# Two convolution layers with group norm: channels on partitions, 32x32 TensorE tiles over pixel pairs

## The chip, the cores and the metric

The kernel runs on one core of one Trainium2 chip. The metric is the device time of one launch in microseconds (us), lower is better. TensorE (PE) multiplies, VectorE (DVE), ScalarE (ACT) and GpSimd (POOL) work beside it, and SyncE (SP) issues transfers. Everything is fp32.

## What is computed

The input is 64 images of 256 x 256 pixels with 16 channels (268 MB). Two layers follow each other; each is a group norm over 8 groups of two channels (statistics over the whole image), a 3x3 convolution whose kernel is a product of small factors, a bias, a relu and a residual sum:

```python
def _L0_conv_ref(inputs, u, v, w, b):
    kern = jnp.einsum('lj,lk,li->ijkl', u, w, v)
    out = lax.conv_general_dilated(inputs, kern, window_strides=(1, 1), padding='SAME', ...)
    return jax.nn.relu(out + b)
...
x = x + _L0_conv_ref(_gn(x), L0_conv_u, L0_conv_v, L0_conv_w, L0_conv_b)
x = x + _L1_conv_ref(_gn(x), L1_conv_u, L1_conv_v, L1_conv_w, L1_conv_b)
```

## The kernel before

The partition is an image row; an image is two halves of 128 rows, and a row holds 256 pixels of 16 channels. Four images lie in SBUF (`image`, 4 MB each). A job is one layer of one image, 128 jobs in all, two images taken in turn, so that the norm of one job is worked out during another. The jobs of a group of four images are written out, and the group is looped over 16 times.

A job has a row stage and a band stage. The row stage has 18 tiles (NT), nine for each half. For a tile, TensorE transposes four windows of eight pixels (L271), so that pixel and channel come onto the partitions; ScalarE applies the norm's scale and bias on the way out of PSUM (L355); TensorE multiplies by `mix`, the horizontal taps and the channel mix (L285); DVE (two tiles of three, L423) or ScalarE (L370) copies the result to `z`. The band stage has 16 products with a 128x128 band matrix over rows, one for each channel, of 512 columns each (L320), whose PSUM ScalarE takes out with relu and bias (L398), and one step of four small rows at the seam between the halves (L314, two products with 64 rows and 32 columns of the array, into neighbouring column groups). Between jobs DVE adds the relu to the image (L434, 16 adds) and takes statistics for the next norm (L445, 16); these fill DVE's queue between the copies of the row stage. A norm ends in a product with ones (L329) and some ten small DVE steps (L459 to L484) with one root on ScalarE (L345).

TensorE's queue is in program order: two tiles' transposes run ahead, then the row step of a tile, then the bands. The PSUM buffers are two for transposes, two for row products and three for bands. At L281 and L269 TensorE's sequencer waits for a buffer by an instruction of its own. An image is loaded in one transfer of 4 MB (L230, L365) and stored in one (L360). An fp32 product or row of the profile is two pairs of weight load and matmul records, a transpose one pair.

Of the kernel before, what the change touches and what calls it, by code (L numbers as in the profile page):

```python
# [8 lines left out]
P = 128  # L29
HALVES = H // P  # L30
GN_GROUPS = 8
EPS = 1e-5
TAPS = 3
LAYERS = 2
PX = P // C
SPAN = PX + 2
BANK = 512
BUFS = 4
JOBS = BUFS * LAYERS
GROUPS = IMAGES // BUFS  # L40

TILES_W = []
_start = 0
while _start < W:
    _windows = [s for s in range(_start, _start + 4 * PX, PX) if s < W]
    _end = _windows[-1] + PX
    TILES_W.append((_start + (_start > 0), W - 1 if _end == W else _end - 2, _windows))
    _start = W if _end == W else _end - 2  # L50
TILES = [(half, *t) for half in range(HALVES) for t in TILES_W]
NT = len(TILES)

T_SLOTS = 3
PS_T, PS_Z, PS_B = 2, 2, 3
LOAD_AT = 6
STORE_AT = 3
EARLY = 2
SEAM_AT = 9
STAT_AT, ROOT_AT = 10, 12  # L60
BANDS = list(range(C))
BANDS.insert(SEAM_AT, "seam")
NB = len(BANDS)
ADD_PX = 32
ADDS = HALVES * W // ADD_PX
STATS = HALVES * GN_GROUPS
FILL_FROM = 3
FILL_A = 24
PARAMS = C + 2 * TAPS * C + C + TAPS + 1
SEAM_PARTS = 2  # L70
SEAM_W = W // SEAM_PARTS


def on_scalar(i):

    return i % 3 == 2


ZA = sum(on_scalar(i) for i in range(NT))
ZV = NT - ZA  # L80


def z_before(i, scalar):

    return sum(on_scalar(n) == scalar for n in range(i + 1))


def layer_of(k):
    return k % 4 // 2


def buf_of(k):
    return 2 * (k // 4) + k % 2


def build(nc, x, params, shifts, spans, seams, pick, out):
# [5 lines left out]
    x_rows = x.rearrange("n (s p) w c -> n p s (w c)", p=P)  # L102
    out_rows = out.rearrange("n (s p) w c -> n p s (w c)", p=P)

    with ExitStack() as ctx:
# [8 lines left out]
        R = sb("relu", [P, C, HALVES, W])  # L114
        T = sb("transposed", [P, T_SLOTS, BANK])
        band = [sb(f"band{y}", [P, C, P]) for y in range(LAYERS)]
        mix = [sb(f"mix{y}", [P, SPAN, C]) for y in range(LAYERS)]
        seam_w = [sb(f"seam_w{y}", [P, P]) for y in range(LAYERS)]
        par = [sb(f"parameters{y}", [P, PARAMS]) for y in range(LAYERS)]
        shift = sb("shift", [P, TAPS, P])  # L120
        span = sb("span", [P, TAPS, SPAN])
        pick_s = sb("pick", [P, 2, GN_GROUPS])
        ones = sb("ones", [P, P])
        seam_z = sb("seam_z", [P, W])
        seam_r = sb("seam_r", [SEAM_PARTS * 2 * C, SEAM_W])
        bn = sb("bn", [P, STATS, 2, 3])
        squares = sb("squares", [P, STATS, 2])
        sums = sb("sums", [P, 2, GN_GROUPS])
        picked = sb("picked", [P, 2, GN_GROUPS])
        moments = sb("moments", [P, 2])  # L130
        small = sb("small", [P, 6])
        norm = sb("norm", [P, 2, 2])

        seam_mask = Z[:, 0:1, :, :].rearrange("p l s w -> p (l s w)")[:, 0:TAPS * P].rearrange(
            "p (i m) -> p i m", i=TAPS)
        z_flat = Z[:, 1:1 + LAYERS, :, :].rearrange("p l s w -> p l (s w)")
        mixed = [z_flat[:, y, 0:TAPS * C].rearrange("p (j l) -> p j l", j=TAPS) for y in range(LAYERS)]
        part = [z_flat[:, y, TAPS * C:(TAPS + SPAN) * C].rearrange("p (q l) -> p q l", q=SPAN)
                for y in range(LAYERS)]
        scratch = [R[:, 4 * y:4 * y + 4, :, :].rearrange("p l s w -> p (l s w)").rearrange(  # L140
            "p (l m) -> p l m", l=C) for y in range(LAYERS)]

        ps_t = [ctx.enter_context(nc.psum_tensor(f"ps_t{i}", [P, BANK], fp32)) for i in range(PS_T)]
        ps_z = [ctx.enter_context(nc.psum_tensor(f"ps_z{i}", [P, BANK], fp32)) for i in range(PS_Z)]
        ps_b = [ctx.enter_context(nc.psum_tensor(f"ps_b{i}", [P, BANK], fp32)) for i in range(PS_B)]
        ps_s = ctx.enter_context(nc.psum_tensor("ps_s", [P, BANK], fp32))

        const_in = sem("const_in")
        image_in = [sem(f"image_in{b}") for b in range(BUFS)]
        image_out = [sem(f"image_out{b}") for b in range(BUFS)]  # L150
        ones_set = sem("ones_set")
        built = sem("built")
        set_step = sem("set_step")
        set_step_pool = sem("set_step_pool")
        turned = sem("turned")
        normed = sem("normed")
        z_made = sem("z_made")
        z_vector = sem("z_vector")
        z_scalar = sem("z_scalar")
        seam_in = sem("seam_in")  # L160
        banded = sem("banded")
        relued = sem("relued")
        seam_out = sem("seam_out")
        added = sem("added")
        stat_step = sem("stat_step")
        stat_sums = sem("stat_sums")
# [400 lines left out]
```

## Time and profile before

| | us |
|---|---|
| median of 3 runs | 5744.07 (5743.53 to 5744.48) |
| the profiled execution | 5745.21 |
| its span, first to last instruction | 5743.4 |
| TensorE busy | 5165.1 (90%) |
| DVE busy | 4424.2 (77%) |
| ScalarE busy | 3427.1 (60%) |

The page gives busy time by engine, the chain of work that ended last, and groups of instructions by line. In a row, x is a count, "mean ns" the recorded length of one (for TensorE with the time until its result has landed, so records overlap), and the idle time is that of the engine just ahead of such instructions, with what ended it. PE is TensorE's matmul, PEld its weight load and PEldq its sequencer.

### The profile page before, as it was taken

The numbers are of one execution on the slowest core, as the hardware profiler recorded it, in microseconds if no ns is written. First come the engines' busy times: TensorE is split into PE (matmuls) and PEld (weight loads), VectorE is DVE, ScalarE is ACT, GpSimd is POOL, SyncE is SP. The second block draws the span as 40 slices with busy tenths as digits, with TensorE's granted clock in tenths as the row PEclk, the third lists the DMA queues.
The fourth block names the chain that finished last, engine by engine and source line by source line (L and its number), as shares of the span: only waits on it lengthen the run. The fifth ranks groups of instructions, "written<-read, shape, count | busy, mean of one in ns | idle before, by whom it ended". The sixth has DMA issues, their size and how long they took to land.

```text
span 5743.4 us, 82893 instructions
## 1 busy us (share of the span) xinstructions
PE 5165.1 (90%) x30976; PEld 3930.7 (68%) x30976; DVE 4424.2 (77%) x7315; ACT 3427.1 (60%) x5377; POOL 26.0 (0%) x25
## 2 busy tenths in 40 slices
PE   6999999999999999999999999999999999999997
PEld 5766676667666766676667666766677666766675
DVE  6777777777777777777777777777777777777776
ACT  4656665566556655665566556655665566556654
POOL 1000000000000000000000000000000000000000
PEclk9999999999999999999999999999999999999999
DMA  3211222122222112221122212222212222212211
GB/s 123 118 63 75 107 120 120 71 82 91 120 120 91 78 74 120 120 102 80 62 120 120 120 62 87 95 120 120 84 71 89 120 120 91 90 62 120 120 61 61
DMA packets 61156, 555.35 MB, mean 97 GB/s; under 512 B 11105, under 2 KB 28001, under 8 KB 28001
## 3 DMA queue, kind: packets, MB, share of 16 engines
q10 hardware_dynamic: 33728, 520.10, 21.9%
q1 hardware_dynamic: 27040, 29.95, 1.7%
q8 instruction: 260, 4.26, 0.3%
q14 instruction: 128, 1.04, 0.1%
HBM read 268.99 MB, written 268.44 MB: 94 GB/s over the span
## 4 chain that ended last, share of the span: by engine, by line
PE 53%; DVE 44%; issue 1%; DMA 1%; ACT 0%; SPq 0%; DVEq 0%; ACTq 0%
DVE image L434 34%; PE ps_b L320 31%; PE ps_z L285 15%; DVE z L423 10%; PE ps_t L271 6%; PE ps_b L314 1%; DMA relu<-seam_r 1%; SPq L244 0%; PE ps_s L329 0%; ACT transposed L355 0%; DMA image<-in_x 0%; ACT relu L398 0%; DVE bn L445 0%; DVE band L210 0%; DVE relu L207 0%
## 5 line engine op out<-in xcount | busy, mean ns | idle before, releaser
L285 PE MATMUL ps_z<-mix,transposed 128*128 128x160 f32 (+2 forms) x17408 | 2566.4, 291 | 488.1 <-DVE z L423 460.1
L285 PEld LDWEIGHTS ps_z<-mix,transposed 128*128 128x128 f32 x17408 | 2317.5, 191 | 636.6 <-ACT transposed L355 349.8
L355 ACT ACTIVATE transposed<-ps_t,norm 128x512 f32<-128x512 f32 (+1 forms) x2304 | 1722.1, 755 | 1075.3 <-PE ps_t L271 1070.5
L434 DVE TENSOR_TENSOR image<-image,relu 128x512 f32<-128x512 f32 x2048 | 2061.1, 1071 | 18.6 <-DMA relu<-seam_r 18.3
L320 PE MATMUL ps_b<-z,band 128*128 128x512 f32 x4096 | 1851.2, 601 | 10.3 <-DVE z L423 0.7
L398 ACT ACTIVATE relu<-ps_b,parameters 128x512 f32<-128x512 f32 x2048 | 1408.4, 688 | 498.8 <-PE ps_b L320 471.4
L423 DVE COPY z<-ps_z 128x480 f32<-128x480 f32 (+1 forms) x1536 | 1031.6, 672 | 779.0 <-PE ps_z L285 778.9
L271 PE MATMUL ps_t<-shift,image 128*128 128x128 f32 x8704 | 1330.1, 273 | 37.0 <-DVE small L217 19.7
L320 PEld LDWEIGHTS ps_b<-z,band 128*128 128x128 f32 x4096 | 748.0, 190 | 858.5 <-issue 819.8
L445 DVE BATCH_NORM_STATS2 bn<-image 128x6 f32<-128x512 f32 x2048 | 1263.6, 715 | 17.3 <-DMA image<-in_x 17.3
L271 PEld LDWEIGHTS ps_t<-shift,image 128*128 128x128 f32 x8704 | 1026.9, 142 | 115.8 <-issue 96.0
L370 ACT ACTIVATE z<-ps_z 128x480 f32<-128x480 f32 (+1 forms) x768 | 392.9, 512 | 678.8 <-PE ps_z L285 678.6
L468 DVE TENSOR_TENSOR picked<-ps_s,pick 128x16 f32<-128x16 f32 x128 | 22.3, 174 | 237.3 <-PE ps_s L329 237.3
L480 DVE TENSOR_SCALAR small<-small 128x1 f32<-128x1 f32 x128 | 34.9, 273 | 205.7 <-ACT small L345 205.7
L329 PEld LDWEIGHTS ps_s<-sums,ones 128*128 128x128 f32 x256 | 48.8, 191 | 72.8 <-issue 60.7
L314 PEld LDWEIGHTS ps_b<-seam_z,seam_w 64*32 64x32 f32 x512 | 18.1, 104 | 97.0 <-ACT relu L398 97.0
L314 PE MATMUL ps_b<-seam_z,seam_w 64*32 64x128 f32 x512 | 52.4, 281 | 0.0
L329 PE MATMUL ps_s<-sums,ones 128*128 128x16 f32 x256 | 37.6, 222 | 11.6 <-DVE sums L464 11.6
L394 ACT ACTIVATE seam_r<-ps_b,parameters 64x128 f32<-64x128 f32 x128 | 44.7, 350 | 0.0
L459 DVE TENSOR_TENSOR squares<-bn 128x32 f32<-128x32 f32 x128 | 28.8, 225 | 4.4
L484 DVE TENSOR_SCALAR norm<-moments,norm 128x1 f32<-128x1 f32 x128 | 27.3, 214 | 4.6
L473 DVE TENSOR_SCALAR small<-moments,small 128x1 f32<-128x1 f32 x128 | 27.4, 214 | 4.6
(38 smaller groups left out, 246.7 us busy)
## 6 DMA issues: line engine op xcount, KB each, us to landing
out<-image ACTq DMA_DIRECT2D x64, 4096.0 KB, 11.3
image<-in_x ACTq DMA_DIRECT2D x60, 4096.0 KB, 13.4
image<-in_x SPq DMA_DIRECT2D x4, 4096.0 KB, 27.6
seam_z<-z SPq DMA_DIRECT2D x256, 32.0 KB
relu<-seam_r SPq DMA_DIRECT2D x512, 8.0 KB, 1.9
shift<-in_shifts SPq DMA_DIRECT2D x1, 192.0 KB, 2.4
z<-in_seams SPq DMA_DIRECT2D x1, 192.0 KB, 2.6
parameters<-in_params SPq DMA_DIRECT2D x2, 66.0 KB, 2.1
```

What stands on the lines that cost most here:

```text
L271: last = nc.tensor.transpose(ps_t[i % PS_T][:, n * P:(n + 1) * P], X[b][:, half, s * C:(s + PX) * C], shift[:, 1, :])
L285: last = nc.tensor.matmul(ps_z[i % PS_Z][:, (a - lo) * C:(z + 1 - lo) * C], T[:, i % T_SLOTS, n * P:(n + 1) * P], mix[layer_of(k)][:, a - ...
L314: part_done = nc.tensor.matmul(ps_b[m % PS_B][2 * C * q:2 * C * (q + 1), 0:SEAM_W], seam_w[y][0:4 * C, 0:2 * C], seam_z[0:4 * C, q * SEAM_ ...
L320: nc.tensor.matmul(ps_b[m % PS_B][:], band[y][:, l, :], Z[:, l, :, :].rearrange("p s w -> p (s w)"), start=True, stop=True).then_inc(bande ...
L329: nc.tensor.matmul(ps_s[:, 0:2 * GN_GROUPS], ones[:], sums[:].rearrange("p a g -> p (a g)"), start=True, stop=True).then_inc(stat_sums, 1)
L355: nc.scalar.activation(T[:, i % T_SLOTS, 0:n], ps_t[i % PS_T][:, 0:n], ACT.Identity, scale=norm[:, k % 2, 0:1], bias=norm[:, k % 2, 1:2]). ...
L370: nc.scalar.activation(Z[:, :, half, lo:hi + 1], ps_z[i % PS_Z][:, 0:(hi + 1 - lo) * C].rearrange("p (q l) -> p l q", l=C), ACT.Identity). ...
L394: nc.scalar.activation(seam_r[:], ps_b[m % PS_B][0:SEAM_PARTS * 2 * C, 0:SEAM_W], ACT.Relu, bias=par[y][0:SEAM_PARTS * 2 * C, PARAMS - 1:P ...
L398: nc.scalar.activation(R[:, l, :, :].rearrange("p s w -> p (s w)"), ps_b[m % PS_B][:], ACT.Relu, bias=par[y][:, at:at + 1]).then_inc(relue ...
L423: nc.vector.tensor_copy(Z[:, :, half, lo:hi + 1], ps_z[i % PS_Z][:, 0:(hi + 1 - lo) * C].rearrange("p (q l) -> p l q", l=C),).then_inc(z_v ...
L434: nc.vector.tensor_tensor(x_ch, x_ch, R[:, :, s, w0:w0 + ADD_PX], ALU.add).then_inc(added, 1)
L445: return nc.vector.bn_stats(bn[:, n, :, :].rearrange("p a b -> p (a b)"), pair)
```

## The change

The kernel is written anew. A channel stays on its partitions through both layers. A partition is (quad of 64 pixel columns, one pixel of a pair, channel): four quads of 32. A column of a tile is an image row, 256 of them. `evens` (N0) holds an image as 33 pixel pairs by 256 rows (with two pad columns), slot 0 being the pair before a quad's first; `odds` (T1, two buffers) holds the output of layer 0, whose pairs are shifted by one pixel; `result` (T2) that of layer 1, pairs as in the input.

- In: four transfers of 32 partitions bring an image to `raw`, 32 rows of each quad on the partitions, and eight DVE block transposes (`turn_in`, 1024 elements for each partition) put it into `evens`. Out: eight of them (`turn_out`) and four transfers.
- The norm's scale goes into the weights (`scale_weights`), its mean into the padding (`pad_evens`, `pad_odds`) and into the bias (`biases`, products of one column). There is no pass that normalises.
- A convolution is eight rounds for each layer and image. A round fills four PSUM banks: 6 taps (two pairs, three rows) and 2 permutations that carry the residual, each as 16 products of 32 rows x 32 columns of the array, 256 columns long, one for each (row group, column group); 128 in a round, 129 in the first of layer 0. ScalarE takes relu and bias of 1024 elements for each partition (`relu`), DVE adds the residual out of the same banks (`evacuate`).
- PSUM is two sets of four banks, handed out in a fixed order (`uses`, `take`). The sums of both norms and the biases are uses of their own: 19 in an image.
- Statistics: ScalarE squares and sums 1024 elements eight times for each image and layer; POOL folds eight chunks of `evens` by seven adds; the sums of layer 1 are taken along with the relu.
- Order: phase A of image p is layer 0 of p, phase B is layer 1 of p-1. In A DVE also turns image p+1 in, in B it turns p-1 out and works out the next two norms. `raw` and `pixels` are single buffers. No loop is left: all of it is written out.

```diff
-        X = [sb(f"image{b}", [P, HALVES, W * C]) for b in range(BUFS)]
-        Z = sb("z", [P, C, HALVES, W])
...
+        raw = sb("raw", [P, HB, RUN])
+        N0 = sb("evens", [P, QUADS * SLOTS + 1, HP])
+        T1 = [sb(f"odds{i}", [P, QUADS, SLOTS + 1, HP]) for i in range(2)]
+        T2 = [sb(f"result{i}", [P, QUADS, H]) for i in range(T2_SLOTS)]
...
+            def load(p):
+                if p:
+                    sp.wait_ge(turned_in, SLOTS * p)
+                for r in range(QUADS):
+                    sp.dma_start(raw[Q * r:Q * (r + 1), :, :], x_quads[p, r]).then_inc(image_in, 16)
...
+            def take(*key):
+                if USE[key] < SETS:
+                    return
+                kind, *of = ORDER[USE[key] - SETS]
+                if kind == "conv":
+                    y, p, e = of
+                    pe.wait_ge(evac1 if y else evac0, ROUNDS * p + e + 1)
+                elif kind == "sum":
+                    pe.wait_ge(moments_read, norms_before(*of) + 1)
...
+            def conv0(p, e):
+                take("conv", 0, p, e)
...
+                for t in range(NTAP):
+                    side, i = t // TAPS, t % TAPS
+                    for q in range(QUADS):
+                        for r in range(QUADS):
+                            at = t if e or q or r else NTAP + 2 + t
+                            nc.tensor.matmul(to[Q * q:Q * (q + 1), r, 0:H],
+                                             w0[Q * r:Q * (r + 1), at * Q:(at + 1) * Q],
+                                             N0[Q * r:Q * (r + 1), SLOTS * q + e + side, i:i + H],
+                                             start=(t == 0), stop=False, skip_group_check=True)
...
+                for side in range(SIDES):
+                    for q in range(QUADS):
+                        for r in range(QUADS):
+                            done = nc.tensor.matmul(to[Q * q:Q * (q + 1), r, H:2 * H],
+                                                    perm[Q * r:Q * (r + 1), side, :],
+                                                    N0[Q * r:Q * (r + 1), SLOTS * q + e + side, 1:1 + H],
+                                                    start=False, stop=(side == 1), skip_group_check=True)
+                done.then_inc(filled, 1)
...
+            for p in range(IMAGES + 1):
+                if p < IMAGES:
+                    for e in range(ROUNDS):
+                        conv0(p, e)
+                for e in range(ROUNDS):
+                    if p:
+                        conv1(p - 1, e)
+                    if e == ODDS_SUM and p < IMAGES:
+                        group_sums(1, p)
+                    if e == EVENS_SUM and p + 1 < IMAGES:
+                        group_sums(0, p + 1)
+                    if e == BIAS and p < IMAGES:
+                        biases(p)
...
+            def turn_in(p, d):
+                dve.wait_ge(image_in, 16 * IN_DMAS * (p + 1))
+                if p:
+                    dve.wait_ge(filled, USE["conv", 0, p - 1, min(d, ROUNDS - 1)] + 1)
+                pixels_in = raw[:].rearrange("p j (q k x) -> p q j k x", q=QUADS, x=Q)[:, :, :, d - 1, :]
+                nc.vector.transpose(N0[:, d::SLOTS, 1:1 + H].rearrange("p q (j h) -> p q j h", h=Q),
+                                    pixels_in).then_inc(turned_in, 1)
+
+            def evacuate(y, p, e):
...
+                to = T2[n % T2_SLOTS][:] if y else T1[p % 2][:, :, e, 1:1 + H]
+                nc.vector.tensor_tensor(to, psum(*key)[:, :, H:2 * H], R[CONV[key] % R_SLOTS][:],
+                                        ALU.add).then_inc(evac1 if y else evac0, 1)
```

## Rows read from the trace of the kernel before

**Rows 1.** The page: busy time by engine; TensorE's granted clock in 40 slices.

```profile
PE 5165.1 (90%) x30976; PEld 3930.7 (68%) x30976; DVE 4424.2 (77%) x7315; ACT 3427.1 (60%) x5377; POOL 26.0 (0%) x25
...
PEclk9999999999999999999999999999999999999999
```

**Rows 2.** Windows: a row stage, the band stage after it; columns as its first line.

```profile
core 0: us, PE busy (x) PEld busy (x) DVE busy (x) ACT busy (x) POOL busy (x), PEclk, DMA share, GB/s
1995.50:2026.40 30.90, 27.05 (x208) 24.77 (x206) 24.92 (x33) 17.31 (x27) 0.00 (x0) 1.00 0.39 155
2026.50:2044.50 18.00, 17.96 (x67) 9.73 (x68) 10.34 (x27) 13.79 (x22) 0.00 (x0) 1.00 0.57 237
```

**Rows 3.** The waits, longest in total: who waited for whom, us, times, longest.

```profile
ACT transposed L355 <- PE ps_t L271: 1070.5, 1154, 15.5
...
DVE z L423 <- PE ps_z L285: 778.9, 391, 3.2
...
PE ps_z L285 <- DVE z L423: 460.1, 604, 1.4
```

**Rows 4.** Timeline of TensorE: start us, length us, records merged.

```profile
2025.87 0.60 PE L271 MATMUL ps_t<-shift,image 128*128 128x128 f32 x4
2026.54 7.96 PE L320 MATMUL ps_b<-z,band 128*128 128x512 f32 x18
2034.43 0.41 PE L314 MATMUL ps_b<-seam_z,seam_w 64*32 64x128 f32 x4
...
2035.73 0.29 PE L329 MATMUL ps_s<-sums,ones 128*128 128x16 f32 x2
```

**Rows 5.** TensorE's weight loads at a seam, from the timeline.

```profile
2920.13 0.14 PEld L314 LDWEIGHTS ps_b<-seam_z,seam_w 64*32 64x32 f32 x4 [0.76 <-ACT relu L398]
```

**Rows 6.** Line 281, the sequencer's own waits, from 2687.3 to 2687.6 us: min/median/max ns.

```profile
L281 PEldq EVENT_SEMAPHORE  x2: 51/51/51, 2687.4 to 2687.5; - x2
```

**Rows 7.** Groups by line and form: busy us, mean ns of one, idle before.

```profile
L434 DVE TENSOR_TENSOR image<-image,relu 128x512 f32<-128x512 f32 x2048 | 2061.1, 1071 | 18.6 <-DMA relu<-seam_r 18.3
...
L445 DVE BATCH_NORM_STATS2 bn<-image 128x6 f32<-128x512 f32 x2048 | 1263.6, 715 | 17.3 <-DMA image<-in_x 17.3
...
L398 ACT ACTIVATE relu<-ps_b,parameters 128x512 f32<-128x512 f32 x2048 | 1408.4, 688 | 498.8 <-PE ps_b L320 471.4 <-DVE image L434 3.1
...
L370 ACT ACTIVATE z<-ps_z 128x480 f32<-128x480 f32 x512 | 299.4, 585 | 255.2 <-PE ps_z L285 255.2
...
L370 ACT ACTIVATE z<-ps_z 128x240 f32<-128x240 f32 x256 | 93.5, 365 | 423.6 <-PE ps_z L285 423.4
...
L210 POOL TENSOR_TENSOR band<-band,relu 128x2048 f32<-128x2048 f32 x2 | 9.1, 4532 | 0.2
...
L210 DVE TENSOR_TENSOR band<-band,relu 128x2048 f32<-128x2048 f32 x2 | 4.6, 2292 | 0.1
...
L216 DVE TENSOR_TENSOR seam_w<-seam_w,z 128x128 f32<-128x128 f32 x2 | 0.6, 291 | 0.1
```

**Rows 8.** Transfers: queue, packets, MB, share of 16 engines; issues with us to landing.

```profile
q8 instruction: 260, 4.26, 0.3%
...
out<-image ACTq DMA_DIRECT2D x64, 4096.0 KB, 11.3
image<-in_x ACTq DMA_DIRECT2D x60, 4096.0 KB, 13.4
...
relu<-seam_r SPq DMA_DIRECT2D x512, 8.0 KB, 1.9
```

**Rows 9.** Timeline of DVE at the start: first statistics, first norm.

```profile
17.28 9.59 DVE L445 BATCH_NORM_STATS2 bn<-image 128x6 f32<-128x512 f32 x16 [17.28 <-DMA image<-in_x]
26.90 3.00 DVE L459 TENSOR_TENSOR squares<-bn 128x32 f32<-128x32 f32 x1
...
35.17 0.21 DVE L484 TENSOR_SCALAR norm<-moments,norm 128x1 f32<-128x1 f32 x1
```

**Rows 10.** Line 329: min/median/max ns, first and last start, form.

```profile
L329 PE MATMUL ps_s<-sums,ones x256: 179/262/395, 30.9 to 5666.9; 128*128 128x16 f32 x128
```

More of the change, by code:

```diff
@@ L29 @@
 P = 128
-HALVES = H // P
+Q = 32
+QUADS = 4
+EPS = 1e-5
 GN_GROUPS = 8
-EPS = 1e-5
 TAPS = 3
-LAYERS = 2
-PX = P // C
-SPAN = PX + 2
-BANK = 512
[L38 to L85, printed above, removed]
@@ L88, in layer_of @@
[L88 to L96, printed above, removed]
+SIDES = 2
+SLOTS = 8
+HP = H + 2
+ROUNDS = SLOTS
+HB = H // Q
+RUN = W // QUADS * C
+BANK = 512
+SETS = 2
+T2_SLOTS = 3
+R_SLOTS = 2
+COUNT = H * W * 2
+NTAP = SIDES * TAPS
+PRM = Q * (1 + SIDES + TAPS) + 1
+CST = Q * (SIDES + SIDES + 1) + 2
+IN_DMAS, OUT_DMAS, HALO0_DMAS, HALO1_DMAS = QUADS, QUADS, 2, 3
+FOLDS = SLOTS - 1
+EVENS_IN_A = {5: (1,), 6: (2,), 7: (3,)}
@@ L97, in build, with norms_before @@
+USE = uses()
+ORDER = list(USE)
+CONV = {key: n for n, key in enumerate(key for key in ORDER if key[0] == "conv")}
+def norms_before(y, p):
+    return 2 * p + y
+def build(nc, x, params, consts, out):
     fp32 = mybir.dt.float32
@@ L120, in build @@
[L120 to L131, printed above, removed]
@@ new lines, in build @@
+        sums = [sb(f"sums{y}", [P, 2]) for y in range(2)]
+        mom = [sb(f"moments{y}", [P, 2]) for y in range(2)]
+        center = [mom[y][:, 0:1] for y in range(2)]
+        small = [sb(f"small{y}", [P, 4]) for y in range(2)]
+        scale = sb("scale", [P, 2])
+        edge = sb("edge", [P, 1])
+        bias = sb("bias", [P, 2])
+        ps = [ctx.enter_context(nc.psum_tensor(f"ps{i}", [P, QUADS, BANK], fp32)) for i in range(SETS)]
+        perm = cst[:, 0:SIDES * Q].rearrange("p (s m) -> p s m", s=SIDES)
@@ new lines, in group_sums @@
+            def group_sums(y, p):
+                take("sum", y, p)
+                pe.wait_ge(reduced1 if y else reduced0, p + 1)
+                to = psum("sum", y, p)
+                for q in range(QUADS):
+                    for r in range(QUADS):
+                        done = nc.tensor.matmul(to[Q * q:Q * (q + 1), r, 0:2], same_group[Q * r:Q * (r + 1), :],
+                                                sums[y][Q * r:Q * (r + 1), :], start=True, stop=True)
+                done.then_inc(filled, 1)
@@ new lines, in bias_of, with biases @@
+            def bias_of(weights, center_y, to, column, first):
+                for q in range(QUADS):
+                    done = nc.tensor.matmul(to[Q * q:Q * (q + 1), 0, column:column + 1],
+                                            weights[0:Q, NTAP * Q:(NTAP + 1) * Q], center_y[0:Q, :],
+                                            start=first, stop=True, skip_group_check=True)
+                return done
+            def biases(p):
+                take("bias", p)
+                to = psum("bias", p)
+                if p >= 0:
+                    pe.wait_ge(scaled1, p + 1)
+                    done = bias_of(w1[p % 2], center[1], to, 0, True)
+                if p + 1 < IMAGES:
+                    pe.wait_ge(scaled0, p + 2)
+                    done = bias_of(w0, center[0], to, 1, p < 0)
+                done.then_inc(filled, 1)
```

726 lines of the change are left out of this document (387 added, 339 removed).

## The prediction

> **What bounds the kernel now.** I read the page's busy shares first: TensorE 90%, DVE 77%, ScalarE 60%, and a full granted clock throughout (2.4 GHz, the upper of its two levels) [rows 1]. The windows say where TensorE's 10% goes. A band stage is full (17.96 of 18.00 us), a row stage is not (27.05 of 30.90 us), and DVE is busy for 24.92 us there [rows 2]. The waits name a loop of TensorE, DVE and ScalarE around the few PSUM buffers of the row stage: ScalarE waits 1070.5 us for transposes, TensorE 460.1 us for DVE's copies [rows 3]. So TensorE's columns are the bound, and in the row stage DVE delays it. What a job costs TensorE: a column of a record costs it the same in every form. Four records of 128 columns take 0.60 us, eighteen of 512 take 7.96 us; the difference, 7.36 us over 8704 columns, is 0.846 ns a column, and what is left is a tail of 0.17 us until the last result has landed [rows 4]. A product with 32 rows and columns would cost as much as a full one if it ran alone. The change stands or falls with whether 16 of them run side by side.
>
> **Evidence on products side by side.** The seam is the only place where parts of the array are used. Its two products (four records of 128 columns, 64 rows by 32 columns of the array, neighbouring column groups, same rows) take 0.41 us [rows 4]. One after another they would take 4 x 0.108 + 0.17 = 0.60 us, as the transposes do; two deep they take 2 x 0.108 + 0.17 = 0.39, with 0.03 for the first weights. The four weight loads, too, lie in 0.14 us [rows 5]. So two column groups do run together, moving operands and weights. Not shown: four row groups together, sixteen tiles, and a stream that never pauses (these four were queued behind a wait of 0.76 us, [rows 5]).
>
> **TensorE after the change.** A round has 128 products, 8 on each of 16 tiles, so 16 records of 256 columns on each tile: 16 x 256 x 0.846 = 3.46 us if all tiles run together. That is the lower bound. A second bound is the sequencer, which now passes 128 x 4 = 512 instructions a round. Two of its waits at L281 start about 0.1 us apart, 2687.4 and 2687.5 us, with a tile's 16 loads and products between them in the program [rows 6]: 0.1 us / 16 = 6 ns for one (under 12 with the rounding), so 3.2 us a round, at most 6.4. The sequencer is thus near the array's own time. I take 3.6 us a round, by the array row and a little for starts, 4.0 as a bad case. The first round of layer 0 has one product more, 2 x 0.217 = 0.43 us.
>
> Stalls come on top. PSUM is two sets in turn. While a round is filled, the one before is emptied by ScalarE's relu, then by DVE's add. The relu of 1024 elements: 512 take 688 ns, and one element more 0.917 ns (585 and 365 ns at 480 and 240), so 1.16 us [rows 7]. The add: 2292 and 291 ns at 2048 and 128 elements give 1.04 ns an element and 158 ns, so 1.22 us [rows 7]. With TensorE's tail and semaphores, about 2.7 us: less than 3.6, so hidden. But three uses in an image (two sums, one bias) take a set and fill nothing. The round after such a use has the set of the round just before it, and waits for the whole emptying: 3 x 2.7 = 8.1 us an image. In sum: 16 x 3.6 + 0.43 + 8.1 = 66.1 us an image, where the kernel before takes 5743.4 / 64 = 89.7.
>
> **What lies beside it.** DVE: 16 adds and 16 block transposes. No row shows a block transpose. Its bounds are 1.22 us (the price of an element at L210) and twice the strided add L434, 2 x 1.07 = 2.14 us [rows 7]; it reads runs of 32 elements, not single ones, so I take 1.22. With one reduction of 1024 elements, some 26 small steps of 0.2 us and 1.0 us of scaling weights: 39.0 + 1.2 + 5.2 + 1.0 = 46.4 us of 66.1, hidden. In phase A it needs 2.44 of 3.6 us a round, so it is not late for the next round. With the dear transpose it is 61 us, still under. ScalarE: 16 relus and 16 squares of 1.16 us, and 2 us of padding and roots: 39 us, hidden; only in the fourth round of phase B it has a relu, two squares and the padding, 4.7 us, which may delay TensorE by 0.5 us. POOL: seven adds of 4.53 / 2 = 2.3 us, 16 us [rows 7], with a phase to spare. The transfers: 4 MB landed in 13.4 and 11.3 us [rows 8]; the load has all of phase B (29 + 8 us), the store all of phase A, though there are only single buffers; at twice the time they would still be hidden. On SP the load stands behind the halo transfers, which wait for the last block transpose of phase A, as does the load itself. The norm's chain (8.3 us from first step to last, [rows 9]) is worked out while the other layer's rounds run.
>
> **Fixed parts.** Start: the first image is there at 17.3 us [rows 9]; POOL follows the block transposes and is done after 2.4 + 7 x 2.3, at 36 us; reduction and norm 8.5, so 45. The first phase B has no rounds and two norms one after another, 17 us. End: a last add, a last transpose and a store, 14 us. Together 76.
>
> **The sum.** 64 x 66.1 + 76 = 4306 us of span, and 2 us around it (5745.21 against 5743.4 in the profiled execution, which lies 1.1 us over the median): 4308, so 4310. Own range of this case: at 3.46 us a round and stalls of 2.4 us, (55.4 + 0.4 + 7.2) x 64 + 76 = 4110; at 4.0 us, 72.5 x 64 + 76 = 4716; with transpose and add both at 2.14 us DVE is the bound, 68.5 + 7.4 = 76 us and some 4 of waiting: 5200. So 4000 to 5250.
>
> The Trainium skill's page "TensorE: Matmul & The Clock Gate" (Part 3, packing small matmuls) gives 10.6 times for 16 tiles of 32x32 at 512 columns, starts 4 ns apart. By that a round would be filled in about the 3.46 us of full overlap, and the trace's pair at the seam points the same way.
>
> **Rivals.**
>
> 1. *TensorE's code cannot be fetched fast enough (slower).* The kernel before fetched 260 pages, 4.26 MB, so 16 KB each, for 61952 records and their waits: 256 instructions a page. A packet's time is 0.003 x 16 x 5743 / 260 = 1.06 us [rows 1, 8]. A round now needs two pages, in 3.6 us; before, a page lasted 22 us. If pages are fetched ahead, a page costs 1.06 us and nothing is seen. If the next is asked for only when one is used up, it costs the packet and a landing, up to 1.06 + 1.9 = 3.0 us [rows 8], a round 6.0 us, and the kernel (96 + 8.5) x 64 + 76 = 6760. It loses from 2.5 us a page: (5744 - 76) / 64 = 88.6, less 8.5, over 32 pages. For it: the number of instructions is eight times that of before. Against it: nothing before shows the length of the queue ahead.
>
> 2. *A pair of load and product has a price in TensorE's order, whatever the tile (slower).* The two records of 16 columns at L329 take 0.29 us, and the second is 262 ns long, so it starts 28 ns after the first, where its columns need 14 [rows 4, 10]. At 28 ns a pair, 256 pairs are 7.2 us a round: (115 + 0.4 + 8.1) x 64 + 76 = 7990. Against it: at the seam two pairs more cost nothing to be seen. It loses from 19.5 ns a pair, 5.0 us a round. The Trainium skill's same page (section on the 56 ns gap) says starts are never closer than about 25 ns; by that rule a round is 6.4 us, and the kernel (102.4 + 8.5) x 64 + 76 = 7170. The seam's row speaks against it for tiles that differ.
>
> 3. *The clock falls (slower).* Three pauses of 2.7 us an image and quarter-filled instructions might bring 1.2 GHz: 7.0 us a round, 7800. Before, it stayed at 1.00 although TensorE idled for over a tenth of a row stage [rows 2].
>
> 4. *Row groups take turns (slower).* Only column groups were seen together. Then a round is 4 x 3.46 = 13.9 us, and the kernel some 14,800.
>
> **How the numbers follow.** Chances: the forecast with its range 0.70; something between it and the time before 0.02; rival 1 0.11, rival 2 0.09, rival 3 0.05, rival 4 0.03. The predicted time is 4310. The range 4000 to 6800 holds the forecast, the stretch between and rival 1: 0.83. A change within 0.2% (11 us) can't be told from none. Faster 0.71, same 0.01, slower 0.28.
>
> **What would show it.** Right: the first and last product of a round 3.5 to 4 us apart; three waits for DVE's add in an image, 2.5 to 3 us each, ahead of the round after a sum or bias; DVE near 70% and ScalarE near 60% busy; block transposes of 1.2 us; granted clock 1.00. Rival 1: gaps in TensorE's stream every 256 instructions, with queue 8 busy all the time. Rival 2: even spacing of 20 ns and more between products on different tiles. Rival 3: a clock of 5 tenths. Rival 4: products of one row group follow each other by 0.2 us. The forecast is wrong, above all, if a round takes over 5.0 us for whatever reason.

## The result and the profile after

| | us |
|---|---|
| median of 4 runs | 9455.65 (9445.61 to 9472.92) |
| before, on the same chip | 5744.27 |
| ratio | 1.646 (95% interval 1.6436 to 1.6493) |
| span of the profiled execution | 9443.8 |

The kernel became slower by 65%. The forecast was 4310 us, faster by 25%. The page of the kernel after, with the busy times (engine, us, share, records), TensorE's granted clock in 40 slices, the queues that brought data and code, and the engines' shares of the chain that ended last:

```profile
span 9443.8 us, 546978 instructions
PE 6294.2 (67%) x267392; PEld 4385.9 (46%) x267392; DVE 2737.5 (29%) x3596; ACT 2399.8 (25%) x3970; POOL 967.3 (10%) x453
PEclk8888888888888888888888888888888888888898
...
q1 hardware_dynamic: 116144, 310.70, 15.4%
q10 hardware_dynamic: 69632, 268.45, 13.6%
q8 instruction: 2090, 34.24, 1.5%
...
PE 66%; issue 28%; DVE 2%; ACT 2%; DMA 0%; POOL 0%; SPq 0%; DVEq 0%; POOLq 0%; ACTq 0%
```

Before, TensorE, DVE and ScalarE were better used [rows 1]; now none is full. 28% of the chain is "issue", time in which TensorE waited for nothing that the profile shows. The code, 260 pages before [rows 8], is 2090 pages: TensorE's 534,784 loads and products (2 x 267,392 records) over 256 are 2089. The clock is lower, too: 0.87 of full speed in place of 1.00. The other engines' work is as forecast, which the groups show (busy us, mean ns of one, idle time ahead and what ended it), beside those of before [rows 7]:

```profile
L469 DVE TENSOR_TENSOR odds<-ps,relu 128x1024 f32<-128x1024 f32 x512 | 627.4, 1225 | 3440.8 <-ACT relu L345 3440.8
L345 ACT ACTIVATE relu<-ps,bias 128x1024 f32<-128x1024 f32 x512 | 570.2, 1114 | 3502.5 <-PE ps L276 3493.9
L208 POOL TENSOR_TENSOR fold<-fold,evens 128x1024 f32<-128x1024 f32 x384 | 838.7, 2184 | 2010.3 <-DVE evens L459 2000.4
L478 DVE STREAM_TRANSPOSE pixels<-result 128x1024 f32<-128x1024 f32 x512 | 631.9, 1234 | 20.9 <-DMA out<-pixels 20.9
L459 DVE STREAM_TRANSPOSE evens<-raw 128x1024 f32<-128x1024 f32 x512 | 625.1, 1231 | 16.6 <-DMA raw<-in_x 16.6
```

DVE waits for ScalarE's relu, and that for TensorE's products. The waits (us in total, times, longest) say what TensorE waits for; their counterpart before was a loop through DVE and ScalarE [rows 3]:

```profile
PEld ps L265 <- issue: 1563.0, 858, 8.6
PEld ps L295 <- issue: 1327.3, 868, 8.3
...
PEld ps L295 <- DVE result L469: 228.3, 107, 2.6
...
PEld ps L265 <- DVE result L469: 156.8, 62, 2.8
```

The waits for DVE's add are the forecast stalls after a sum or a bias. The much larger ones for "issue" are new. TensorE's timeline (start, length in us, records, idle time ahead), first in a quiet stretch, then in one where an image is loaded:

```profile
3999.75 2.75 PE L265 MATMUL ps<-evens,scaled 32*32 32x256 f32 x128 [0.97 <-issue]
4003.50 0.45 PE L265 MATMUL ps<-evens,scaled 32*32 32x256 f32 x8 [0.99 <-issue]
...
4007.24 2.75 PE L265 MATMUL ps<-evens,scaled 32*32 32x256 f32 x128 [0.97 <-issue]
4010.99 0.45 PE L265 MATMUL ps<-evens,scaled 32*32 32x256 f32 x8 [0.99 <-issue]
...
4021.62 2.75 PE L295 MATMUL ps<-odds,scaled 32*32 32x256 f32 x128 [0.97 <-issue]
4030.85 0.68 PE L295 MATMUL ps<-odds,scaled 32*32 32x256 f32 x9 [6.48 <-issue]
```

A pause comes after every 128 pairs of load and product, 256 instructions, one page of code. The pauses end at 3999.75, 4003.50, 4007.24 and 4010.99 us, 3.75 us apart; the next ones, up to 4021.62, are 3.4 to 3.7 us apart. During the load the next page takes 9.2 us. Windows of the quiet stretch and of two load bursts (TensorE, its weight loads, DVE, ScalarE, POOL, clock, DMA share, GB/s):

```profile
3996.00:4020.00 24.00, 18.83 (x879) 12.95 (x887) 8.26 (x7) 9.89 (x19) 7.53 (x4) 1.00 0.04 10
4021.00:4043.00 22.00, 10.25 (x353) 7.00 (x355) 4.58 (x10) 4.52 (x9) 0.21 (x1) 0.68 0.94 193
4103.00:4124.00 21.00, 7.68 (x274) 5.02 (x289) 4.29 (x4) 2.79 (x6) 2.00 (x1) 0.77 0.92 193
```

At 3.75 us a page 353 products need 10.3 us; they took 22. So this burst costs 11.7 us (the second, by the same reckoning, 13.0), and there are 128 of them, a load and a store for each of 64 images. The clock falls inside the bursts, where TensorE stands idle, and stays full in the quiet stretch with its pause of about a microsecond a page.

### The profile page after: what moved, and what is told of

It is laid out like the page before. It is cut to its first block, busy times and chain, and to the rows that moved or that the text cites. A ratio compares the mean times of both kernels' runs of the same rounds, so it can differ in the third digit from the quotient of the medians.

```text
span 9443.8 us, 546978 instructions
## 1 busy us (share of the span) xinstructions
PE 6294.2 (67%) x267392; PEld 4385.9 (46%) x267392; DVE 2737.5 (29%) x3596; ACT 2399.8 (25%) x3970; POOL 967.3 (10%) x453
## 3 DMA queue, kind: packets, MB, share of 16 engines
q8 instruction: 2090, 34.24, 1.5%
## 4 chain that ended last, share of the span: by engine, by line
PE 66%; issue 28%; DVE 2%; ACT 2%; DMA 0%; POOL 0%; SPq 0%; DVEq 0%; POOLq 0%; ACTq 0%
PE ps L295 25%; PE ps L265 25%; PE ps L276 8%; PE ps L302 8%; DVE result L469 2%; ACT relu L348 2%; PE ps L231 0%; DMA raw<-in_x 0%; POOL fold L208 0%; PE ps L237 0%; DVE evens L459 0%; ACT junk L335 0%; DVE sums L492 0%; PE ps L270 0%; DVE small L505 0%
## 5 line engine op out<-in xcount | busy, mean ns | idle before, releaser
L265 PE MATMUL ps<-evens,scaled 32*32 32x256 f32 x98304 | 2616.4, 429 | 1324.5 <-issue 1174.0
L295 PE MATMUL ps<-odds,scaled 32*32 32x256 f32 x98304 | 2612.8, 428 | 1155.9 <-issue 938.8
L265 PEld LDWEIGHTS ps<-evens,scaled 32*32 32x32 f32 x98304 | 1639.3, 109 | 2051.8 <-issue 1563.0
L295 PEld LDWEIGHTS ps<-odds,scaled 32*32 32x32 f32 x98304 | 1650.3, 109 | 1887.7 <-issue 1327.3
L469 DVE TENSOR_TENSOR odds<-ps,relu 128x1024 f32<-128x1024 f32 x512 | 627.4, 1225 | 3440.8 <-ACT relu L345 3440.8
L345 ACT ACTIVATE relu<-ps,bias 128x1024 f32<-128x1024 f32 x512 | 570.2, 1114 | 3502.5 <-PE ps L276 3493.9
L348 ACT ACTIVATE relu<-ps,bias 128x1024 f32<-128x1024 f32 x512 | 570.0, 1113 | 2887.5 <-PE ps L302 2859.2
L302 PE MATMUL ps<-odds,constants 32*32 32x256 f32 x32768 | 1060.8, 413 | 262.0 <-issue 261.1
L276 PE MATMUL ps<-evens,constants 32*32 32x256 f32 x32768 | 1085.0, 413 | 201.4 <-issue 201.1
L208 POOL TENSOR_TENSOR fold<-fold,evens 128x1024 f32<-128x1024 f32 x384 | 838.7, 2184 | 2010.3 <-DVE evens L459 2000.4
L478 DVE STREAM_TRANSPOSE pixels<-result 128x1024 f32<-128x1024 f32 x512 | 631.9, 1234 | 20.9 <-DMA out<-pixels 20.9
L459 DVE STREAM_TRANSPOSE evens<-raw 128x1024 f32<-128x1024 f32 x512 | 625.1, 1231 | 16.6 <-DMA raw<-in_x 16.6
## 6 DMA issues: line engine op xcount, KB each, us to landing
raw<-in_x SPq DMA_DIRECT2D x256, 1024.0 KB, 15.1
out<-pixels ACTq DMA_DIRECT2D x256, 1024.0 KB, 13.2
```

The costliest lines, as they stand in the source:

```text
L208: nc.gpsimd.tensor_tensor(fold[:], chunk(1) if d == 2 else fold[:], chunk(d), ALU.add).then_inc(folded, 1)
L265: nc.tensor.matmul(to[Q * q:Q * (q + 1), r, 0:H], w0[Q * r:Q * (r + 1), at * Q:(at + 1) * Q], N0[Q * r:Q * (r + 1), SLOTS * q + e + side, ...
L276: done = nc.tensor.matmul(to[Q * q:Q * (q + 1), r, H:2 * H], perm[Q * r:Q * (r + 1), side, :], N0[Q * r:Q * (r + 1), SLOTS * q + e + side, ...
L295: nc.tensor.matmul(to[Q * r:Q * (r + 1), q, 0:H], w1[p % 2][Q * q:Q * (q + 1), t * Q:(t + 1) * Q], t1[Q * q:Q * (q + 1), r, e + side, i:i ...
L302: done = nc.tensor.matmul(to[Q * r:Q * (r + 1), q, H:2 * H], perm[Q * q:Q * (q + 1), side, :], t1[Q * q:Q * (q + 1), r, e + side, 1:1 + H] ...
L345: ins = nc.scalar.activation(to, got, ACT.Relu, bias=bias[:, 0:1], accum_out=acc_relu[:, e:e + 1])
```

## Theories

*Code*: TensorE is paced by the fetching of its pages, 3.75 us each, whatever the instructions do, and longer while a deep queue of data stands in the way. *Array or clock*: the tiles overlap less than forecast, or the lower clock stretches them, and the pauses only reflect that. *Price of an instruction*: each pair costs TensorE a fixed time. The experiments take columns away, then transfers, then instructions, and then measure each cost alone.

## Experiments

**Columns taken away.** The same instructions, most of them with 32 columns:

```diff
+                    N = H if t == 0 else 32
...
-                            nc.tensor.matmul(to[Q * q:Q * (q + 1), r, 0:H],
+                            nc.tensor.matmul(to[Q * q:Q * (q + 1), r, 0:N],
```

> Same products, same instructions, fewer columns: in each round only the first tap and the first permutation keep 256 columns, the other six products of a tile have 32 (part of the convolution and of the residual is left out). A tile streams 1408 columns a round in place of 4096. If code pages set the pace (one page of 256 TensorE instructions in flight, 3.7 us each): no change, 9300 to 9500 us. If the columns set it: about 4700 us. If a fixed 17 ns for each pair of load and product sets it: 5000 us.

Measured 9402.7 us, 0.6% under the changed kernel (9455.65). A tile streams 1408 columns in a round in place of 4096. The page shows the clock at about half:

```profile
PE 5055.5 (54%) x267392; PEld 3712.1 (39%) x267392; DVE 2737.3 (29%) x3596; ACT 2399.5 (26%) x3970; POOL 963.6 (10%) x453
...
PEclk6555555555555555555555555555555555555555
```

The mean clock is 0.54, where the changed kernel had 0.87. The two changes can't cancel: a third of the columns (1408 of 4096) at 0.54 in place of 0.87 would still need only 55% of the array's time. Taken together they change the time by 0.6%. The array and the clock are not what bounds this kernel.

**Transfers taken away.** Only the first image is loaded and only the last stored:

```diff
-                if p + 2 < IMAGES:
-                    load(p + 2)
...
-                        if e == 1 and p >= 2:
-                            store(p - 2)
```

> Only the first image is loaded and only the last stored; everything else runs as before on the same image (63 loads and 63 stores are left out). If a page's fetch is slowed by the image transfers (9 to 10 us in place of 3.7 while one runs), the excess of 1580 us goes: 2090 x 3.7 + 130 = 7860 us. If the transfers have no part in it: 9440 us. The halves of the gaps over 4.5 us between page fetches should be gone, the 3.7 us should stay.

Measured 8000.67 us, a ratio of 1.3927 (1.3899 to 1.3955) to the kernel before. The longest wait for "issue" at the taps falls from 8.6 us to about 3:

```profile
PEld ps L262 <- issue: 1063.2, 820, 3.1
PEld ps L292 <- issue: 893.3, 762, 2.3
```

The transfers cost 1455 us (9455.65 - 8000.67), 11.4 us for each of 128 bursts, as the window said. What is left is again the page: in this run's trace half of queue 8's page packets start within 3.75 us of the one before, 2090 x 3.75 = 7838 us, and the forecast's 76 for start and end make 7914 of 8001. That leaves 87 us for the stalls for PSUM, of which the taps alone have 413 us in total, 188 times (255.8 and 156.8 us, both for DVE's add). So they hardly add to the time; that pages arrive during them would explain it, but no run tests this.

**TensorE alone, straight code against a loop.** The same products as stretches of 80 waves (a wave is one product on each of 16 tiles) written out, and of 81 waves in a loop; then 32 and 512 columns, and four tiles on the diagonal:

```diff
+            for t in range(80):
+                for q, r in tiles:
+                    nc.tensor.matmul(*at(t, q, r, 256), start=True, stop=True)
+            with pe.Fori(0, 27):
+                for t in range(3):
+                    for q, r in tiles:
+                        nc.tensor.matmul(*at(t, q, r, 256), start=True, stop=True)
```

> TensorE alone, nothing but products on 16 tiles of 32x32 (the layers are left out; a piece of the output is written). A wave is 16 products, 64 instructions, 4 waves are a page. Seven stretches: 80 waves of 256 columns straight, 81 in a loop of 3 waves (its code stays in place), the same with 32 columns, the same with 512, and 1296 products on the four diagonal tiles in a loop. If pages set the pace: 73 us straight with 256 and with 32 columns, 75 to 80 with 512. In the loops no page is fetched: by the array alone 35, 5 and 70 us for 256, 32, 512 columns; with 8.3 ns for an instruction 43 us for 32 columns and 43 to 53 for 256. Diagonal tiles by the array: 140 us.

Its timeline of TensorE (L48 is 256 columns straight, L52 the loop; L55 and L59 the same with 32 columns; L62 and L66 with 512; L71 the four tiles):

```profile
14.35 2.75 PE L48 MATMUL ps<-data,taps 32*32 32x256 f32 x128 [0.54 <-issue]
18.09 2.75 PE L48 MATMUL ps<-data,taps 32*32 32x256 f32 x128 [0.99 <-issue]
...
81.55 49.91 PE L52 MATMUL ps<-data,taps 32*32 32x256 f32 x2496 [0.79 <-issue]
...
147.47 1.54 PE L55 MATMUL ps<-data,taps 32*32 32x32 f32 x128 [1.91 <-issue]
151.20 1.54 PE L55 MATMUL ps<-data,taps 32*32 32x32 f32 x128 [2.19 <-issue]
...
201.58 34.09 PE L59 MATMUL ps<-data,taps 32*32 32x32 f32 x2592
235.58 82.39 PE L62 MATMUL ps<-data,taps 32*32 32x512 f32 x2554
...
317.82 83.54 PE L66 MATMUL ps<-data,taps 32*32 32x512 f32 x2581
...
401.02 139.99 PE L71 MATMUL ps<-data,taps 32*32 32x256 f32 x2587
```

This shows the cause. Straight code of 256 columns goes in pages 3.4 to 4.0 us apart; with 32 columns the products of a page take 1.5 us instead of 2.75 and the pause grows by as much, so the period hardly changes (3.74 and 3.59 us on average). That also says that a page comes in while the one before is worked off: asked for only when that one is used up, it would make the period 1.2 us shorter at 32 columns. The loop, whose code stays in place, has no pauses: 2496 records in 49.9 us. And straight code of 512 columns, where the four waves of a page take 4.1 us, has none either (82.39 us for 2554 records). The straight stretches of 256 and 32 columns came as expected (73.6 and 70.4 us for 73); that of 512 took 82 for 75 to 80. The loops took longer than expected: by the array alone 35, 5 and 70 us were expected, by 8.3 ns for an instruction 43 to 53 and 43 us for 256 and 32 columns. Measured were about 53, 34 and 84.

So the run shows a second thing. A wave of 256 columns takes 49.91 / 78 = 0.64 us (0.65 over the whole stretch, which holds a pause for a page). The four tiles on the diagonal, which share neither rows nor columns, take 0.433 us a wave (139.99 us for 323). So sixteen tiles side by side run at 67% of that. With 512 columns a wave takes 1.03 us, where the columns need 0.87. The 5184 instructions of the 32-column loop take 34.1 us, 6.6 ns each. The clock in the straight stretch of 32 columns and in the loop behind it is 0.50 (window, columns as above without ScalarE):

```profile
147.00:217.00 70.00, 38.05 (x3106) 34.41 (x3107) 0.00 (x0) 0.00 (x0) 0.50 0.01 4
```

**The instructions halved.** A product covers two pixel pairs, 512 columns, so a layer has four rounds of the same 128 products; taps and permutations have four PSUM banks each. Sums and biases stand between the two, so the order of the PSUM uses changes as well. The kernel computes all of the reference. The core of the edit:

```diff
-ROUNDS = SLOTS
+ROUNDS = SLOTS // 2
...
-                            nc.tensor.matmul(to[Q * q:Q * (q + 1), r, 0:H],
-                                             w0[Q * r:Q * (r + 1), at * Q:(at + 1) * Q],
-                                             N0[Q * r:Q * (r + 1), SLOTS * q + e + side, i:i + H],
...
+                                done = nc.tensor.matmul(to[Q * q:Q * (q + 1), r, :],
+                                                        w0[Q * r:Q * (r + 1), t * Q:(t + 1) * Q],
+                                                        N0[Q * r:Q * (r + 1), at:at + 2, i:i + H],
```

> The whole computation with half the instructions: a product covers two pixel pairs, 512 columns; the convolution fills four PSUM banks and the permutations the other four; sums and biases stand between them. 1073 pages in place of 2090. If pages set the pace: 1073 x 3.7 = 3970 us and up to 1580 us from the transfers, 5550 us. If only the array's columns count: 16 x 3.46 + 3 us an image, 3900 us in all. If the price were one of the tiles running side by side (so many columns in so many tiles), no gain: 9400 us.

Measured 6205.86 us, ratio 1.0791 (1.0771 to 1.0812): a third less than the changed kernel, yet still behind the kernel before, and over the highest time expected, 5550. Its code and its largest wait for code:

```profile
q8 instruction: 1073, 17.58, 1.2%
...
PEld ps L274 <- issue: 710.9, 858, 7.3
```

Half the pages are there, but waits for code up to 7.3 us are, too. The next kernel takes the transfers out of this one.

> The kernel with 512 columns a product, with only the first image loaded and the last stored (63 loads and stores left out). 1073 pages at 3.7 us are 3970 us and lie behind the products: by the stretch of 512 columns in a loop a wave of 16 products takes 1.03 us, 64 waves an image, 4230 us, with waits 4300 to 4600. If the transfers are what separates 6206 us from that, this run is there; if waits for PSUM are, it stays near 6200.

The edit is the one that took the transfers out above. Measured 4826.85 us, ratio 0.8402 (0.8385 to 0.8419). So the transfers cost 1379 us here. Without them the array sets most of the pace: 64 waves an image x 1.03 us x 64 = 4219 us of 4821. The 600 us above that, which put the run over its expected 4300 to 4600, are not traced to a wait; the page's busy share:

```profile
PE 4524.9 (94%) x137088; PEld 2755.6 (57%) x137088; DVE 2683.0 (56%) x3084; ACT 2273.7 (47%) x3202; POOL 972.1 (20%) x453
```

**The changed kernel with small transfers.** Same bytes, but each image in pieces of 128 KB, four (512 KB) at a time, one such step in a round:

```diff
-                for r in range(QUADS):
-                    sp.dma_start(raw[Q * r:Q * (r + 1), :, :], x_quads[p, r]).then_inc(image_in, 16)
+                for j in range(HB):
...
+                        sp.wait_ge(filled, USE["conv", 1, p - 3, j] + 1 - (j == 0))
+                    for r in range(QUADS):
+                        sp.dma_start(raw[Q * r:Q * (r + 1), j, :], x_quads[p, r, :, j]).then_inc(image_in, 16)
```

> The changed kernel with its image transfers in pieces of 512 KB, one for each round (loads in phase B, stores in phase A). One fetch in two meets a piece. If a piece delays a fetch by at most its own length, 2.6 us: 64 x 16 x up to 2.6 = up to 2660 us of excess in place of 1580, 9400 to 10500 us. If the delay comes from deep queues only: below 9000 us.

Measured 8223.45 us, ratio 1.4315 (1.427 to 1.436). Of the 1455 us that transfers cost, 1232 are gone though every byte still moves. So the delay comes from how the data is queued, hardly from its amount. The page price remains.

**Which transfers delay a page.** TensorE runs straight waves of 32 columns, and SyncE loads beside it in five ways, one after another: a 4 MB image in four transfers of 1 MB; the same in one transfer of 16 KB rows; 128 KB pieces, one in flight; two in flight; four issued at once, then a wait for all.

> TensorE alone with straight code, products of 32 columns on 16 tiles, five stretches of 40 pages; SyncE loads images beside it (results are not used). Quiet: 3.5 us a page. (1) four transfers of 1 MB at once, packets of 4 KB, as in the changed kernel: 9 to 10 us a page while they run. (2) one transfer of 4 MB with packets of 16 KB, as in the kernel before: as slow or slower, if the fetch waits behind packets in number and size. (3) pieces of 128 KB, one in flight: 4 us. (4) the same, two in flight: 5 us. (5) four pieces at once, then a wait: 6 us. If only the load's bytes matter, all five cost the same for each MB.

The timeline in the first way, then windows before any load, in ways 1 and 2, across 3 and 4, and in way 5 (columns again without ScalarE):

```profile
42.08 1.54 PE L90 MATMUL ps<-data,taps 32*32 32x32 f32 x128 [2.47 <-issue]
51.57 1.53 PE L90 MATMUL ps<-data,taps 32*32 32x32 f32 x128 [7.95 <-issue]
60.78 1.53 PE L90 MATMUL ps<-data,taps 32*32 32x32 f32 x128 [7.68 <-issue]
64.23 1.53 PE L90 MATMUL ps<-data,taps 32*32 32x32 f32 x128 [1.92 <-issue]
```

```profile
10.00:39.00 29.00, 12.28 (x1048) 11.27 (x1040) 0.00 (x0) 0.00 (x0) 1.00 0.02 5
40.00:130.00 90.00, 17.44 (x1467) 16.07 (x1469) 0.00 (x0) 0.00 (x0) 1.00 0.91 188
235.00:288.00 53.00, 13.81 (x1152) 12.69 (x1152) 0.00 (x0) 0.00 (x0) 1.00 0.78 315
401.00:662.00 261.00, 101.26 (x8448) 93.07 (x8448) 0.00 (x0) 0.00 (x0) 1.00 0.23 69
712.00:778.00 66.00, 24.15 (x2033) 22.28 (x2035) 0.00 (x0) 0.00 (x0) 1.00 0.44 129
```

A record count over 128 is the number of pages: one in 3.5 us when quiet, 7.9 in the first way, 5.9 in the second, 4.0 across the third and fourth, 4.2 in the fifth, which still moves 129 GB/s. Two of the expectations failed: the single transfer of 4 MB is not as slow as the four of 1 MB, and four pieces at once cost 4.2 us a page and not 6.

A page's period is not yet the price of a load, since the ways differ in how long they take. What a window holds beyond 3.54 us for each of its pages, divided by its images of 4 MB (4, 4, 4 and 2), is about 12 us for an image in the first way, 5 in the second, 7 across the third and fourth and 5 in the fifth. So the single transfer, with a deep queue and 315 GB/s, delays the code as little for each image as the short queues do. The short queue is one remedy. The second way, which differs from the first in packets of 16 KB for 4 KB and in one transfer for four, looks like another; which of its two differences does it, and whether it helps the changed kernel, was not tried.

**512 columns with short queues.** Two forms of the kernel with halved instructions. First two pieces of 128 KB in flight, issued by SyncE:

```diff
+            def paced(p, chunk, landed):
+                half = QUADS * HB // 2
+                for n in range(QUADS * HB):
+                    if n >= 2:
+                        sp.wait_ge(landed[n % 2], 16 * (half * p + n // 2))
+                    sp.dma_start(*chunk(n % QUADS, n // QUADS)).then_inc(landed[n % 2], 16)
```

> The whole computation, 512 columns a product, the image transfers cut into 32 pieces of 128 KB each way, all issued by SyncE, never more than two in flight. If a page's fetch suffers from what is queued ahead of it on the DMA engines, short queues leave it near 4 to 5 us and the kernel takes 4600 to 5300 us, faster than 5744. If every byte delays the fetches alike, 6200 us as without pacing. If pieces are too slow (over 50 us for an image), the transfers become the bound, 6500 us or more.

Measured 5543.72 us, ratio 0.9639 (0.962 to 0.9659). The chain that ended last is now the transfers themselves:

```profile
DMA 75%; PE 12%; SPq 6%; DVE 3%; issue 2%; ACT 1%; DVEq 0%; ACTq 0%
```

That is over the 5300 expected at most. With two pieces in flight they take too long, and DVE waits for them (620.3 us before it turns an image out, 275.5 before it turns one in). So the second form has four at once:

```diff
+                for j in range(HB):
+                    if j:
+                        sp.wait_ge(landed, 16 * QUADS * (HB * p + j))
+                    for r in range(QUADS):
+                        sp.dma_start(*chunk(r, j)).then_inc(landed, 16)
```

> As the paced kernel with 512 columns, but four pieces of 128 KB at once and then a wait for all four. By the fifth stretch of the micro kernel an image takes 33 us in place of over 40, and a page 4.2 us while it does. If the paced kernel was held by its slow transfers (three quarters of its chain), 4900 to 5200 us, near the 4827 us without transfers. If it was the page fetches, 5500 us still.

Measured 5084.6 us, ratio 0.8853 (0.8839 to 0.8868). It beats both kernels and computes the whole reference. Transfers and SyncE's queue still hold 46% of the chain, and 258 us lie between it and the kernel without transfers:

```profile
PE 4600.1 (91%) x137088; PEld 2764.3 (54%) x137088; DVE 2684.0 (53%) x3084; ACT 2278.3 (45%) x3202; POOL 972.8 (19%) x453
...
PE 32%; DMA 24%; SPq 22%; DVE 12%; issue 6%; ACT 2%; POOL 0%; DVEq 0%; ACTq 0%; POOLq 0%
```

**How tiles overlap.** Loops of 1440 products of 256 columns, in turn over 8 tiles of two column groups (L49), 12 tiles (L53), 16 in the order of layer 0 (L57) and of layer 1 (L61), 16 with three products of a tile in a row (L65), and 8 tiles of two row groups (L69).

> TensorE alone, products of 256 columns in loops whose code stays in place (the layers are left out); 48 products a pass, 30 passes, 1440 products in each stretch, on: 8 tiles (two column groups), 12 tiles, 16 tiles in the order of layer 0, 16 tiles in the order of layer 1, 16 tiles with three products of a tile one after another, and 8 tiles (two row groups). By the array alone a product costs its tile 0.43 us: 78, 52, 39, 39, 39 and 78 us. If 64 instructions are all that can be ahead, 16 tiles cost 0.65 us a wave (58 us), 12 tiles less than 0.5 (60 us) and 8 tiles 0.43 (78 us), and three in a row on one tile cost much more, up to 620 us if nothing else can pass. If the price is one for each instruction, 12 tiles cost 0.49 us a wave (58 us).

```profile
4.70 80.06 PE L49 MATMUL ps<-data,taps 32*32 32x256 f32 x2880 [4.70 <-DMA taps<-in_x]
84.53 63.36 PE L53 MATMUL ps<-data,taps 32*32 32x256 f32 x2880
147.62 56.94 PE L57 MATMUL ps<-data,taps 32*32 32x256 f32 x2880
204.25 56.99 PE L61 MATMUL ps<-data,taps 32*32 32x256 f32 x2880
260.94 221.94 PE L65 MATMUL ps<-data,taps 32*32 32x256 f32 x2876
...
483.19 77.61 PE L69 MATMUL ps<-data,taps 32*32 32x256 f32 x2857
```

A wave takes 0.44 us with 8 tiles (180 waves), 0.53 with 12 (120) and 0.63 with 16 (90). Up to eight tiles cost what four cost, 0.433. From there each tile adds 21 to 26 ns. Row groups overlap as column groups do, and the two orders are alike. Twelve tiles took longer than either assumption of the expectation gave (60 and 58 us). Products of one tile in a row, though, hold back the other tiles: 222 us for the work that takes 57 in turn. In the trace of L57 half of the starts lie within 17 ns of the one before, and a pause of some 120 ns stands about once in a wave. What the 21 to 26 ns are stays open.

## Why the prediction was wrong

**The step that failed: the code (rival 1, mis-sized).** The forecast took the sequencer's 512 instructions a round as passing at 6 ns each, 3.2 us. That price was right: 6.6 ns in the loop at a clock of 0.50, and at 1.00 beside the loads a page of 32 columns took as long (1.53 us against 1.54). What it left out was where instructions come from. Rival 1 named the mechanism, and its sign in the profile, gaps every 256 instructions, is what is there. It was judged unlikely, and its worst case was 3.0 us a page, from a packet of 1.06 us and a landing of 1.9 [rows 1, 8]. Measured were 3.75 us in a quiet stretch and 9.2 us in a burst. The rival's two cases were a page fetched ahead at 1.06 us, with nothing to be seen, and a page asked for late at 3.0 us. The straight stretches show neither: pages come in during the work, and still only one in 3.75 us. By its formula two pages make 7.5 us of a round and the kernel (120 + 8.5) x 64 + 76 = 8300 us; 8001 were measured without transfers, and the bursts bring it to 9456. The landing of a small data transfer was no bound for the time between pages. The rival's other sign did not come: queue 8 is not busy all the time. Its packets take 0.015 x 16 x 9444 / 2090 = 1.08 us of the 3.75, so what costs is the time between pages, not the bandwidth. Why it is 3.75 us stays open, and no run changed how pages are fetched. The argument against the rival, that nothing before showed the length of the queue ahead, was no evidence. A page before lasted 22 us, six times what it takes to get one, so the trace of before could not have shown the price. A resource whose use grows eightfold is unproven, not free, and deserved far more than 0.11.

The Trainium skill's page "Runtime: NRT & Kernel Launch" (Instruction fetch mechanics) says that the sequencer fetches the next 16 KiB page while it executes the current one, and that crossing into it is mostly hidden. Its 16 KiB agree with the 256 instructions between pauses here, and fetching during the work is what the two straight stretches show. "Hidden" held before, where a page lasted 22 us and the trace has no product that waits for issue; it does not hold where one is used up in 2.75 us.

**The term that was mis-sized: the round of the array.** Forecast 3.46 us for full overlap, 3.6 taken, 4.0 as a bad case. The loops give 8 x 0.63 to 0.64 = 5.1 us. The evidence was a pair of column groups [rows 4], and up to eight tiles it holds; it was extended to sixteen. With free code the kernel would then take (16 x 5.1 + 8.5) x 64 + 76 = 5840 us, and with the measured stalls of 2.3 us 5770: estimates from the loops' waves. The forecast's own break-even is 5.0 us a round. So even without the first error the forecast gain of 25% was gone, with a time about the same as before; whether a little faster or slower, these estimates don't decide. This second error is of the array, not of code.

The Trainium skill's page "TensorE: Matmul & The Clock Gate" (Part 3) gave 10.6 times for sixteen tiles, and the prediction read this as full overlap. By 10.6 of 16 a round is 128 x 0.433 / 10.6 = 5.2 us, an estimate from the page's figure and near the loops' 5.1. That is in part luck: the page's figure is for 512 columns, and there the loop here gives 0.84 x 16 = 13.4 times.

**What hid behind it: the transfers.** They were costed at nothing with the rounds as cover, and even at twice their time. A piece of 1 MB landed after 15.1 us in and 13.2 us out, and an image, four pieces at 193 GB/s in the bursts, takes about 22 us, where the forecast had 13.4 and 11.3 for the 4 MB [rows 8]. This is still within twice the time, and DVE waited for the data once each way (16.6 and 20.9 us). But they stood in the way of the code, for 1455 us. A transfer that no engine waits for can still delay the fetching of code.

**The other steps.**

- Stalls after a sum or bias: forecast three in an image of 2.7 us. The trace shows 169 of 192 as waits for DVE's add, (228.3 + 156.8) / 169 = 2.3 us each. The mechanism was right. They hardly add to the time of the kernel without transfers (see there).
- DVE, ScalarE, POOL: add 1.225 us (1.22 forecast), block transpose 1.23 (1.22, and far from the bound of 2.14), relu 1.11 (1.16), POOL's add 2.18 (2.3). The shares are lower than forecast only because the span is longer.
- Rival 2 (28 ns a pair): wrong in size. Pairs pass in 13.2 ns at 32 columns (34.09 us for 2592) and in 19.8 to 20 ns at 256 (56.94 for 2880, 49.91 for 2496). It is no fixed price: at 512 columns it is 32 ns (83.54 for 2581). The 20 ns lie just past its turning point of 19.5, which is the round of 5.1 us again.
- Rival 3 (clock): the clock fell, to 0.68 in a burst, but as a consequence. At about half of it (0.54) the time was the same, with a third of the columns, while the code was the bound.
- Rival 4 (row groups in turn): wrong. Eight tiles in two row groups take 77.6 us, and in two column groups, with all four row groups, 80.1.

## What to carry over

Count instructions of a change as a resource of its own: divide them by 256 and compare the time in which the engine uses up a page with 3.75 us. The 3.75 us are of straight code on TensorE without image transfers beside it. Wider instructions and short DMA queues turned this layout from 1.65 to 0.885 of the time before, with the same arithmetic. Where a trace shows a resource only at an eighth of its new use, it does not bound the new price, so measure it alone before building on it. Overlap seen for two tiles is no evidence for sixteen.

## What the hardware showed that was not expected

- TensorE gets a page of 256 instructions of straight code every 3.4 to 4.0 us, whether its products have 32 columns or 256. A load of 4 MB in four queued transfers beside it makes this 9 to 10 us for two pages of three; 128 KB pieces, four at a time, only 4.2. For each image the delay is about 12 us in the first way and 5 in the last, and 5 with one transfer of 4 MB in packets of 16 KB.
- Sixteen tiles of 32x32 in turn run at 67% of full overlap at 256 columns and 84% at 512 (0.87 / 1.03); eight run at 97%.
- Three products in a row on one tile make a stream over sixteen tiles 3.9 times as long (221.94 / 56.94).
- The same straight code of 32 columns ran at a granted clock of 0.50 (1.2 GHz) in the first kernel of TensorE alone and at 1.00 (2.4 GHz) beside the loads. The period of its pages was 3.6 and 3.5 us. What the engine did just before differs: a stretch of 256 columns there, nothing here. More about the clock was not tried.
